# Layer-1 probabilities transposed by quarter moves and 32x32 VectorE transposes

## What is computed

```python
# layer 0: group norm, attention of 8 heads, projection, group norm, residual
hn = group_norm(x, gn1_scale, gn1_bias)
q, k, v = split(w_qkv @ hn + b_qkv)                # per head 64 channels
a = softmax((q*s).T @ (k*s)) applied to v
x = x + group_norm(w_proj @ a + b_proj, gn2_scale, gn2_bias)
# layer 1: one head over all 512 channels
qkv = w_qkv1 @ x ; qkv = qkv / (sqrt(mean(qkv**2, channels)) + 1e-4)
attn = softmax(q.T @ k * 512**-0.5)                # [1024, 1024] per image
h = w_out @ (v @ attn.T)
out = (x + h) * 2**-0.5
```

## Time and profile before

| | us |
|---|---|
| median of 3 runs | 3530.38 (3525.94 to 3533.14) |
| the profiled execution, own time | 3528.0 |
| its span, first to last instruction | 3526.2 |
| TensorE busy | 3462.6 (98%) |
| VectorE busy | 2077.1 (59%) |
| ScalarE busy | 1825.4 (52%) |
| GpSimd busy | 1083.3 (31%) |

### The profile page before, as it was taken

How to read it: one execution, slowest core, us unless ns; L and a number is a source line. 1 busy time by engine, 2 the same in 40 slices (tenths; PEclk the granted TensorE clock), 3 DMA queues, 4 the chain that set the end, 5 groups by cost and what they waited for, 6 DMA issues and landing times.

```text
span 3526.2 us, 52658 instructions
## 1 busy us (share of the span) xinstructions
PE 3462.6 (98%) x17360; PEld 2835.9 (80%) x17360; DVE 2077.1 (59%) x3388; ACT 1825.4 (52%) x3074; POOL 1083.3 (31%) x947
## 2 busy tenths in 40 slices
PE   7999999999999999999999999999999999999999
PEld 3888788887888788887878878788787887888878
DVE  4677446773377734786347854478444884457742
ACT  3577126762278522784237832378323882247822
POOL 0245213442034410354104531145211452114521
PEclk9999999999999999999999999999999999999999
DMA  8512215312244113341033311342203422142210
GB/s 310 157 39 58 108 43 138 74 48 84 66 115 96 41 69 97 85 96 72 36 121 81 76 72 43 114 96 61 84 37 109 96 61 84 43 133 65 60 48 24
DMA packets 63520, 294.41 MB, mean 83 GB/s; under 512 B 9201, under 2 KB 9457, under 8 KB 52465
## 3 DMA queue, kind: packets, MB, share of 16 engines
q1 hardware_dynamic: 63216, 290.65, 28.1%
HBM read 158.49 MB, written 31.46 MB: 54 GB/s over the span
## 4 chain that ended last, share of the span: by engine, by line
PE 87%; issue 6%; DVE 3%; ACT 2%; POOL 2%; DMA 0%; SPq 0%; ACTq 0%; DVEq 0%; POOLq 0%
PE big L430 29%; PE tps L529 14%; PE big L556 12%; PE ops L542 12%; PE ops L702 10%; PE big L626 6%; PE big L473 1%; PE ops L430 1%; ACT PB L827 1%; PE big L594 1%; DVE XA L1247 1%; POOL XA L967 1%; DVE HL L1252 0%; DVE small L1175 0%; PE big L465 0%
## 5 line engine op out<-in xcount | busy, mean ns | idle before, releaser
L957 POOL TENSOR_SCALAR PB<-PB,small 128x1024 f32<-128x1024 f32 x576 | 648.1, 1126 | 1304.3 <-DVE small L1181 1293.4
L833 ACT ACTIVATE PT<-tps 128x512 fp32r<-128x512 f32 x1088 | 601.2, 597 | 251.7 <-PE tps L529 248.5
L1186 DVE TENSOR_TENSOR PT<-tps,PT 128x512 fp32r<-128x512 f32 x1088 | 693.1, 678 | 39.0 <-ACT PT L833 38.6
L1175 DVE TENSOR_REDUCE small<-big 128x1 f32<-128x1024 f32 x512 | 624.8, 1220 | 63.2 <-PE big L556 59.9
L529 PEld LDWEIGHTS tps<-ident,PB 128*128 128x128 f32 x4608 | 527.1, 140 | 125.0 <-DVE PT L1186 56.0
L529 PE MATMUL tps<-ident,PB 128*128 128x128 f32 x4608 | 618.0, 275 | 8.9 <-DVE PT L1186 6.1
L827 ACT ACTIVATE PB<-big,small 128x1024 f32<-128x1024 f32 x512 | 572.2, 1118 | 73.1 <-DVE small L1175 70.2
L542 PE MATMUL ops<-PT,VT 128*128 128x512 f32 x2048 | 599.3, 415 | 0.0
L556 PE MATMUL big<-ST 128*128 128x512 f32 x2048 | 555.4, 393 | 10.9 <-ACT PB L827 10.9
L556 PEld LDWEIGHTS big<-ST 128*128 128x128 f32 x2048 | 382.1, 188 | 101.8 <-ACT PB L827 19.9
L542 PEld LDWEIGHTS ops<-PT,VT 128*128 128x128 f32 x2048 | 346.2, 189 | 47.0 <-DVE PT L1186 5.0
(11 more groups left out here) (157 smaller groups left out, 4659.2 us busy)
## 6 DMA issues: line engine op xcount, KB each, us to landing
ST<-ST SPq DMA_DIRECT2D x384, 256.0 KB, 4.9
W<-d_qk SPq DMA_DIRECT2D x32, 1024.0 KB, 5.2
XA<-in_x SPq DMA_DIRECT2D x8, 2048.0 KB, 7.7
X<-in_x SPq DMA_DIRECT2D x8, 2048.0 KB, 10.6
W<-d_wp SPq DMA_DIRECT2D x8, 2048.0 KB, 12.2
W<-d_g SPq DMA_DIRECT2D x8, 2048.0 KB, 12.2
W<-d_m SPq DMA_DIRECT2D x8, 2048.0 KB, 7.7
W<-d_u SPq DMA_DIRECT2D x8, 2048.0 KB, 10.3
```

What stands on the lines that cost most here:

```text
L833: act_fn(pt_slot(u, s)[:, 0, :], tps[n % 2][:], ACT.Copy).then_inc(s_pt_hi, 1)
L957: nc.gpsimd.tensor_scalar(PB[:, i, :], PB[:, i, :], rinv[:, i:i + 1], 1.0, ALU.mult, ALU.mult)\
L1175: V.tensor_reduce(negmax[:, i:i + 1], tile(("s", 4 * u + tb))[:], axis=AX.X, op=ALU.max, negate=True).then_inc(s_row_max, 1)
L1186: V.tensor_tensor(pt_slot(u, s)[:, 1, :], tps[n % 2][:], pt_slot(u, s)[:, 0, :].bitcast(f32), ALU.subtract).then_inc(s_pt_ready, 1)
```

## The change

- The columns of the layer-1 score tiles, of RB and so of PB are in another order: column 256q+32s+r holds key 128s+32q+r (`by_quarter`). The moving operand of `scores1` is read in pieces of 32 columns for that.
- When the four probability tiles of half c are normalised, SP issues 16 moves of 128 KB from PB to F, a view of W[0]: quarter tq of the partitions and quarter sq of the columns go to partition quarter sq. VectorE then turns 128x512 blocks of F in 32x32 blocks into PB (`turn`, eight for each half), which gives the transposed probabilities. High and low part are made from there (`turned_hi` on ScalarE, `turned_lo` on VectorE) and no longer from `tps`.
- TensorE has no transposes in layer 1. It does the eight score tiles in one go, then all values. The mean product stands behind score tile 5 and writes `tps[0]`, the variance product behind tile 6 and writes `tps[1]`; "gna" and "gnb" are gone from `BIG`.
- VectorE's order: maxima 4, 5, 6, the deviations, six turns, two low halves, maximum 7, two turns, the other low halves; then coefficients and `norm_f32`, `layer_out(0)`, `layer_out(1)`, `norm_lo`, the eight turns of half 1, `layer_out(2)`, four low halves, `layer_out(3)`, the rest.
- SP: the `d_wv` load moves behind the turns of half 1 and behind the first three stores.

```diff
+QUARTERS = 4
+EXCHANGE = QUARTERS * QUARTERS * 16
...
+        F = W[0][:, :].bitcast(f32).rearrange("p (q t n) -> p q t n", q=QUARTERS, t=KB)
+        def turned(c, s):
+            return PB[:, 4 * c + s // 2, HALF * (s % 2):HALF * (s % 2) + HALF]
+        def by_quarter(row):
+            return row.rearrange("p (s q r) -> p q s r", q=QUARTERS, s=NT)
... SP
-                    sp.wait_ge(s_big_full, big_count(b, ("u", NT - 1)))
+                for c in range(2):
+                    sp.wait_ge(s_p_norm, b * 72 + 64 + 4 * c + 4)
+                    if c:
+                        sp.wait_ge(s_e_ready, b * 16 + 8)
                     own_wait(sp)
-                    sp.dma_start(W[0][:].bitcast(f32), d_wv[:]).then_inc(s_ld_wv, 16)
+                    for tq in range(QUARTERS):
+                        for sq in range(QUARTERS):
+                            sp.dma_start(F[32 * sq:32 * sq + 32, tq, :, :],
+                                         PB[32 * tq:32 * tq + 32, 4 * c:4 * c + 4, 256 * sq:256 * sq + 256])\
+                              .then_inc(s_exchanged, 16)
                 for j in range(8):
+                    if j == 3 and not last:
+                        sp.wait_ge(s_e_ready, b * 16 + 16)
+                        own_wait(sp)
+                        sp.dma_start(W[0][:].bitcast(f32), d_wv[:]).then_inc(s_ld_wv, 16)
... TensorE
-                                             lambda h, k: x1(h, k)[:, cols], range(KB))
+                                             lambda h, k: by_quarter(x1(h, k))[:, 2 * half:2 * half + 2], range(KB))
...
+                    elif (c, e) == (0, 3):
+                        last.then_inc(s_slot_read, 1)
...
-                for i in range(4):
+                for i in range(NT):
                     scores1(i)
+                    if i == 5 and not last_batch:
+                        group_means(GN_PER_BATCH * (b + 1) + 1, tps[0][:, 0:KB], every, None, s_gn1_full)
+                    if i == 6 and not last_batch:
+                        group_vars(GN_PER_BATCH * (b + 1) + 1, tps[1][:, 0:KB], every, s_gn1_full)
                 pe.wait_ge(s_vp_ready, b * 8 + 8)
                 for c in range(2):
-                    for tb in range(4):
-                        if c == 0:
-                            scores1(4 + tb)
-                        if (c, tb) != (1, 0):
-                            transposes(UNITS0 + c, 2 * tb)
-                            transposes(UNITS0 + c, 2 * tb + 1)
...
+                    for s in range(NT):
+                        values1(c, 0, s)
+                        values1(c, 1, s)
                     for e in (2, 3):
-                        for s in range(8):
-                            if (c, e, s) == (0, 3, 6):
-                                transposes(UNITS0 + 1, 0)
-                                transposes(UNITS0 + 1, 1)
+                        for s in range(NT):
                             values1(c, e, s)
... ScalarE
+                def turned_hi(c, s):
+                    act.wait_ge(s_e_ready, b * 16 + 8 * c + s + 1)
+                    if c and s < 7:
+                        act.wait_ge(s_slot_read, b * 7 + s + 1)
+                    elif c:
+                        act.wait_ge(s_o_full, b * 24 + UNITS0 + 4 + CREDIT)
+                    act_fn(pt_slot(UNITS0 + c, s)[:, 0, :], turned(c, s), ACT.Copy).then_inc(s_pt_hi, 1)
+                for i in range(7):
                     exps1(i)
+                for s in range(6):
+                    turned_hi(0, s)
+                exps1(7)
+                turned_hi(0, 6)
+                turned_hi(0, 7)
+                if not last_batch:
+                    norm_hi(b + 1)
+                for s in range(NT):
+                    turned_hi(1, s)
... VectorE
-                V.tensor_copy(RB[:], tile(("r", 0))[:]).then_inc(s_r_ready, 1)
+                V.tensor_copy(RB[:].rearrange("p (q s r) -> p q s r", q=QUARTERS, s=NT), by_quarter(tile(("r", 0))[:]))\
+                 .then_inc(s_r_ready, 1)
...
+                def turn(c, s):
+                    if s == 0:
+                        dve.wait_ge(s_exchanged, (2 * b + c + 1) * EXCHANGE)
+                    V.transpose(turned(c, s).rearrange("p (t q r) -> p t q r", t=KB, q=QUARTERS),
+                                F[:, :, :, 32 * s:32 * s + 32].rearrange("p q t r -> p t q r")).then_inc(s_e_ready, 1)
+                def turned_lo(c, s):
+                    dve.wait_ge(s_pt_hi, b * 144 + 8 * (UNITS0 + c) + s + 1)
+                    slot = pt_slot(UNITS0 + c, s)
+                    V.tensor_tensor(slot[:, 1, :], turned(c, s), slot[:, 0, :].bitcast(f32), ALU.subtract)\
+                     .then_inc(s_pt_ready, 1)
+                scaled_max(4)
+                recip1(4)
+                scaled_max(5)
+                recip1(5)
+                scaled_max(6)
+                if not last_batch:
+                    dve.wait_ge(s_gn_mean, GN_PER_BATCH * (b + 1) + 1)
+                    dve.wait_ge(s_gn1_full, b * 2 + 1)
+                    group_dev(tps[0][:, 0:KB], mv[:, :, 0], every)
+                recip1(6)
+                for s in range(6):
+                    turn(0, s)
+                turned_lo(0, 0)
+                turned_lo(0, 1)
+                scaled_max(7)
+                if not last_batch:
+                    dve.wait_ge(s_gn1_full, b * 2 + 2)
+                    group_veps(tps[1][:, 0:KB], every)
+                turn(0, 6)
+                turn(0, 7)
+                turned_lo(0, 2)
+                turned_lo(0, 3)
+                recip1(7)
+                for s in range(4, NT):
+                    turned_lo(0, s)
+                if not last_batch:
+                    group_coefs(GN_PER_BATCH * (b + 1) + 1, gs1, gb1, every).then_inc(s_dve_step, 1)
+                    links[1] += 1
+                    dve.wait_ge(s_dve_step, links[0] + links[1])
+                    norm_f32()
                 layer_out(0)
                 layer_out(1)
                 if not last_batch:
-                    dve.wait_ge(s_dve_step, links[0] + links[1])
-                    norm_f32()
+                    norm_lo(b + 1)
+                for s in range(NT):
+                    turn(1, s)
                 layer_out(2)
-                if not last_batch:
-                    norm_lo(b + 1)
-                pt_lo(UNITS0 + 1, 0)
-                pt_lo(UNITS0 + 1, 1)
-                layer_out(3)
-                for s in range(2, NT):
-                    pt_lo(UNITS0 + 1, s)
+                for s in range(NT):
+                    if s == 4:
+                        layer_out(3)
+                    turned_lo(1, s)
```

More of the change, by code:

```diff
@@ L66 @@
 BIG += [("y", 0), ("y", 1), ("y", 2), ("y", 3), ("u", 0), ("u", 1), ("u", 2), ("r", 0)]
-BIG += [("u", s) for s in range(3, NT)] + [("s1", t) for t in range(6)]
-BIG += [("gna", 1), ("s1", 6), ("gnb", 1), ("s1", 7)]
+BIG += [("u", s) for s in range(3, NT)] + [("s1", t) for t in range(NT)]
 NBIG = len(BIG)
@@ L71 @@
 HI = [key for key in BIG if key[0] in ("v", "qk", "y", "u")]
-BIG_LAST = [key for key in BIG if key not in (("gna", 1), ("gnb", 1))]
 SETUP_BIG = 3 * KB
@@ L232, in build @@
         s_coef_b = sem("coef_b")
+        s_gn1_full = sem("gn1_full")
         s_gn2_full = sem("gn2_full")
@@ L242, in build @@
         s_sum_full = sem("sum_full")
+        s_exchanged = sem("exchanged")
+        s_e_ready = sem("e_ready")
+        s_slot_read = sem("slot_read")
         s_ms_done = sem("ms_done")
@@ L290, in big_at @@
         def big_at(b, key):
-            return (BIG_LAST if isinstance(b, int) else BIG).index(key)
+            return BIG.index(key)
         def big_count(b, key):
@@ L705, in values1 @@
                         last.then_inc(s_o_full, 1)
+                    elif (c, e) == (0, 3):
+                        last.then_inc(s_slot_read, 1)
                 pe.wait_ge(s_y_ready, b * 4 + 4)
-                for i in range(4):
+                for i in range(NT):
                     scores1(i)
+                    if i == 5 and not last_batch:
+                        group_means(GN_PER_BATCH * (b + 1) + 1, tps[0][:, 0:KB], every, None, s_gn1_full)
+                    if i == 6 and not last_batch:
+                        group_vars(GN_PER_BATCH * (b + 1) + 1, tps[1][:, 0:KB], every, s_gn1_full)
                 pe.wait_ge(s_vp_ready, b * 8 + 8)
                 for c in range(2):
-                    for tb in range(4):
-                        if c == 0:
-                            scores1(4 + tb)
-                        if (c, tb) != (1, 0):
-                            transposes(UNITS0 + c, 2 * tb)
-                            transposes(UNITS0 + c, 2 * tb + 1)
-                        if tb:
-                            for s in (2 * tb - 2, 2 * tb - 1):
-                                values1(c, 0, s)
-                                values1(c, 1, s)
-                        if (c, tb) == (0, 1) and not last_batch:
```

(48 more changed lines are left out.)

7 lines of the change are left out of this document (3 added, 4 removed).

## The result

| | before | after |
|---|---|---|
| median of the runs, us | 3528.16 (4 runs) | 3582.40 (3579.79 to 3583.66, 4 runs) |
| ratio to before | | 1.0151, 95% interval 1.0138 to 1.0163 |
| span of the profiled execution, us | 3526.2 | 3578.0 |
| mean granted TensorE clock | 0.998 | 0.988 |

The forecast was 3534 within 3503 to 3598.

A forecast was written before the change was run, and what follows sets the result against it. TensorE's matmul queue, busy 98%, was taken as the bound. Waits of 8.6 us against 8.1 removed give +0.5 a batch, about +4 in all: 3534 us, range 3503 to 3598.

The forecast's parts named there:

- transposes removed: TensorE's layer 1 without its 64 transposes: 8.1 us a batch can be had.
- 1 variance product: Behind score tile 6, TensorE waits for VectorE's deviations, which stand behind that tile's maximum: 2.2 us.
- 2 first value: After score tile 7, TensorE waits for the first low half, behind exp 6 and six turns: 0.4 us.
- 3 low halves 2, 3: TensorE waits for low half 2 (1.0, 0.1 to restart) and low half 3, which meets GpSimd's normalisation (0.3): 1.4 us.
- 4 layer_out(0): TensorE waits for its ops tile, as coefficients and four scalings now stand ahead of layer_out(0): 2.2 us.
- 5 first value of half 1: TensorE waits for half 1's first low half, behind norm_lo, eight turns and layer_out(2): 0.6 us.
- 5 second group, layer_out(3): Half 1's second value group waits for layer_out(3), which stands behind four low halves: 1.8 us.
- 32-column pieces: Score matmuls reading in 32-column pieces: taken as 0; slower matmuls, 5% or 2.2 us a batch, had chance 0.05.
- rival A: Slower: the exchange sets the second half; 3572 at 16 us of exchange, 3652 at 21 us; chance 0.13.
- The turn: VectorE's 32x32 transposes of a 128x512 block: taken as 0.62 us each, trace mean expected near 0.68.
- B: Slower: turns of two passes; 3596 at 1.15 us a turn, 3556 at 0.8; chance 0.10.
- the prediction's own sign: Prediction counts as wrong if layer 1 of a batch is more than 3 us from 95.9.

The follow-up runs named there:

- x3: The changed kernel with only 8 of the 16 moves in each image's second exchange; 3546.42 us, ratio 1.0043 to the kernel before.
- x1: The changed kernel with unread matmuls (7, 12 and 7 an image) put into three of TensorE's waits; 3555.75 us, ratio 1.0075 to the kernel before.
- y3: The changed kernel with GpSimd's normalisation of probability row 6 ahead of its wait for maximum 7; 3576.07 us, ratio 1.0130 to the kernel before.
- z2: The changed kernel with VectorE's turns and low halves laced, variance product behind tile 7, normalisation 6 early and four moves on ScalarE's queue; 3530.71 us.
- z5: As z2, with VectorE's order refitted to its trace, such as layer_out(0) and layer_out(1) behind the first scaling; 3546.54 us.
- x2: The changed kernel with the score matmuls' moving operand read in straight columns instead of pieces of 32; 3556.63 us, ratio 1.0083 to the kernel before.
- y4: The changed kernel with variance product behind tile 7, layer_out(3) behind the first low half, four moves on ScalarE's queue and normalisation 6 early; 3527.15 us.

## Why the prediction was right or wrong

One image's layer 1 takes 102.7 us (2602.16 to 2704.87) instead of 95.4 (2568.55 to 2663.94): +7.3. It is not the same in every image (eight times 7.3 would be 58): from one image's last value matmul to the next one's the change costs 5.7 to 7.8 us in seven images, least where the kernel before has a half-clock stretch in layer 0, and 3.5 in the last, which has no products for a next image; together the 51.8 between the profiled executions. The steps of this image:

| step | predicted us | measured us |
|---|---|---|
| transposes removed | -8.1 | -7.1 |
| 1 variance product | 2.2 | 1.84 |
| 2 first value | 0.4 | 0 |
| 3 low halves 2, 3 | 1.4 | 0.78 |
| 4 layer_out(0) | 2.2 | 0.55 |
| 5 first value of half 1 | 0.6 | 3.12 |
| 5 second group, layer_out(3) | 1.8 | 1.79 |
| layer_out(4) | 0 | 0.33 |
| 32-column pieces | 0 | 1.9 |
| half clock behind the waits | no term | 1.6 + 2.5 |
| sum | +0.5 | +7.3 |

The measured waits are differences of starts in the timeline above, less the matmuls in between; the half clock is 7.28 us for score tile 7 (2644.34 to 2651.62) less 5.68, and the 2.5 of the 21 matmuls. The first row is eight groups of 0.89. My 8.1 was layer 1's length less its score and value matmuls, and so held 1.0 us of small products and breaks besides, which stay: less its matmuls, transposes, waits and half clock, layer 1 keeps 1.2 us in the kernel before and 1.3 in the change.

- **The waits.** Their sum is 8.4 against my 8.6: the mechanism and the places were right. That the sums agree so closely is luck, since single terms are off by up to 2.5. Within the sum the second exchange was too cheap (13.3 us for 12.2, and begun at t=33.9 instead of 31.6, since tile 7 ends later), and so the second half waits 3.1 and not 0.6. Each move cost 0.70 us of SP's time and not the 0.59 that I had taken from the stack moves' bytes. The earlier waits were too dear, since slower score tiles and the half clock bring TensorE there later. x3 shows that the exchange ends last; rival A's mechanism was at work at 13.3 us.
- **The clock: the step that failed.** The sum had no term for what TensorE does after a wait. It is 4.1 us in this image, 27 us in all by x1. The earlier trace rows could not show it, since TensorE of before had hardly a wait in layer 1. But the trace of before had it in layer 0. There TensorE waits 1.83 us in each image (L626), and behind that wait the clock is at half in three of the eight. First the wait of image 1, then the stretches behind the same wait in images 0 and 1:
```profile
795.68 0.56 PE L626 MATMUL big<-HH,W 128*128 128x512 f32 x1 [1.83 <-DVE HL L1252]
```
```profile
366.20:369.70 3.50, 3.50 (x16) 1.00 0.10 9
795.99:799.40 3.41, 3.41 (x9) 0.50 0.06 10
```
I never asked what the engine's first microseconds behind a wait of 2 us cost; a mean clock of 0.998 hid it.
- **The 32-column pieces.** "I take 0" was mis-sized: 4.2% on the score matmuls, 15 us, just under the bound of 5% that I had kept as a rival with a chance of 0.05.
- **The turn** has a mean of 677 ns and a pitch of 0.61, as taken. VectorE's low halves and GpSimd's normalisations do hold each other up, by 0.8 us a meeting (y3) where I had taken 0.3, and they meet at low halves 4 to 7 and not at 3.
- **The range and the direction.** The time lies in the range partly by luck: its upper part came from an exchange of up to some 18 us (A) and turns of two passes (B), and it was 13.3 us and 0.61. By the prediction's own sign, a layer 1 more than 3 us from 95.9, its timetable was wrong: 102.7. The exchange too ended 2.84 us behind the norm's low halves, and not with them. Slower had a chance of 0.44, more than faster (0.32), but the time named was that of no change.

## What to carry to other kernels

Before an instruction is taken off an engine that is always busy, list the waits it leaves and price each twice: its length, and the time at the lower clock that may follow it; look for such stretches in other parts of the trace first. Where a wait can't be taken away, dummy work in it can pay (x1), and of two orders with the same sum of waits the one with the waits spread out was the faster (z2 against z5). An exchange through many small moves has an issue rate as well as a byte rate; read both from the nearest row. When a schedule of several engines gains nothing from a new order, look for the stretch whose length stays the same: here 28 us in z2 and z5, from tile 7 through exponent, normalisation, exchange and turns.

## What the runs showed that I had not expected

- The granted clock was at half for 3.4 us behind a wait of 1.70 us in five images of the change, and for 6.8 us behind the two waits of the second half in all eight (2.96 and 1.40 us in the image shown, with three matmuls between them). It stayed full behind the same wait of 1.70 us in the other two images, in all seven of x2, and behind one of 1.69 us in y4, with 0.59 and 1.23 us waits to come. What tells these cases apart stays open; no rule is drawn from them.
- 26 matmuls an image without a purpose (19 in the last) made the change 27 us faster.
- A moving operand read in pieces of 32 float32r columns takes 0.236 us for 512 columns instead of 0.227.
- A move of 128 KB from 32 to 32 partitions in pieces of 1 KB takes 0.607 us to issue on SP (16 of them 11.2 us) and 2.4 us to land.
- VectorE's 32x32 float32 transposes of 128x512 take 0.61 us in a row, as an elementwise operation of that size.
